# Final normalisation gathered behind the pair loop, score transposes behind the weighting, more value pairs split in an attention kernel

## What is computed

```python
H_l = H @ W_l
H_r = H @ W_r
S = H_l @ H_r.T                  # 4096 x 4096
beta = softmax(S, axis=-1)
B = beta @ H
O = B @ W_h @ W_g
x = layernorm(x + adj @ H + gamma * O)   # H is x
```

## Time and profile before

| | us |
|---|---|
| median of 3 executions | 1307.47 (1305.02 to 1307.64) |
| the profiled execution, its own time | 1307.26 |
| its span in the profile | 1305.4 |
| PE busy | 1259.0 (96%) |
| DVE busy | 958.2 (73%) |
| ACT busy | 800.9 (61%) |
| POOL busy | 233.7 (18%) |
| GpSimd remainders `ring_lo`, 64 | 155.4 |
| exponentials, 128 | 134.2 |
| rounded weights `p_hi` (L897), 64 | 67.9 |

### The profile page before, as it was taken

How to read it: one execution, slowest core, us unless ns; L and a number is a source line. 1 busy time by engine, 2 the same in 40 slices (tenths; PEclk the granted TensorE clock), 3 DMA queues, 4 the chain that set the end, 5 groups by cost and what they waited for, 6 DMA issues and landing times.

```text
span 1305.4 us, 17888 instructions
## 1 busy us (share of the span) xinstructions
PE 1259.0 (96%) x6139; PEld 829.7 (64%) x6139; DVE 958.2 (73%) x1265; ACT 800.9 (61%) x966; POOL 233.7 (18%) x136
## 2 busy tenths in 40 slices
PE   8999999989999899999999999999999999999987
PEld 3566666643332334788888888886677776767764
DVE  7987987720000556899999898978878888878885
ACT  1334555511110224788888777867978778788795
POOL 0100000000000000001010000012334333354355
PEclk9999999989999899999999999999999999999999
DMA  9877766589999699999999999960000000000000
GB/s 366 317 272 295 288 238 241 206 334 354 359 344 409 251 390 388 311 369 386 371 379 367 366 352 382 363 248 1 1 1 1 1 1 1 1 19 15 1 1 32
DMA packets 82816, 294.33 MB, mean 225 GB/s; under 512 B 9658, under 2 KB 11322, under 8 KB 82746
## 3 DMA queue, kind: packets, MB, share of 16 engines
q1 hardware_dynamic: 80496, 292.59, 59.7%
q10 hardware_dynamic: 2250, 0.82, 0.2%
HBM read 291.27 MB, written 2.10 MB: 225 GB/s over the span
## 4 chain that ended last, share of the span: by engine, by line
PE 85%; DVE 6%; DMA 4%; ACT 3%; issue 2%; DVEq 0%; SPq 0%; ACTq 0%
PE acc L1612 9%; PE acc L1607 9%; PE acc L1608 9%; PE acc L1694 8%; PE acc L1546 8%; DMA raw<-in_adj_s 4%; PE acc L1460 4%; PE acc L1452 3%; PE acc L1456 3%; PE acc L1453 3%; PE acc L1684 2%; PE acc L1688 2%; PE acc L1685 2%; PE rs L1469 2%; PE e L1649 2%; PE rs L1651 2%
## 5 line engine op out<-in xcount | busy, mean ns | idle before, releaser
L1161 DVE TENSOR_TENSOR t_lo<-raw,t_hi 128x1024 fp32r<-128x1024 f32 x256 | 303.2, 1230 | 21.6 <-ACT t_hi L847 18.2
L847 ACT ACTIVATE t_hi<-raw 128x1024 fp32r<-128x1024 f32 x256 | 261.5, 1054 | 38.0 <-PE acc L1612 36.9
L1607 PE MATMUL acc<-t_hi,st_hi 128*128 128x512 f32 x512 | 201.9, 394 | 0.6 <-ACT t_hi L847 0.6
L1608 PE MATMUL acc<-t_hi,st_lo 128*128 128x512 f32 x512 | 199.6, 390 | 0.0
L682 POOL TENSOR_TENSOR ring_lo<-ring,p_hi 128x1024 fp32r<-128x1024 f32 x64 | 155.4, 2429 | 231.3 <-ACT p_hi L897 231.2
L1612 PE MATMUL acc<-t_lo,st_hi 128*128 128x512 f32 x512 | 158.9, 392 | 1.4 <-DVE t_lo L1161 1.1
L1246 DVE TENSOR_TENSOR ring<-ring,e 128x1024 f32<-128x1024 f32 x128 | 153.9, 1210 | 0.1
L891 ACT ACTIVATE ring<-ring 128x1024 f32<-128x1024 f32 x128 | 134.2, 1054 | 23.1 <-DVE ring L1246 22.6
L637 POOL COPY xb<-x 128x512 f32<-128x512 f32 (+1 forms) x24 | 32.3, 1345 | 588.5 <-DVE xs L1079 214.8
L1694 PE MATMUL acc<-ring,x 128*128 128x512 f32 x256 | 120.4, 592 | 0.0
L1612 PEld LDWEIGHTS acc<-t_lo,st_hi 128*128 128x128 f32 x512 | 95.0, 188 | 24.6 <-DVE t_lo L1161 4.8
(11 more groups left out here) (228 smaller groups left out, 2181.2 us busy)
## 6 DMA issues: line engine op xcount, KB each, us to landing
raw<-in_adj_s SPq DMA_DIRECT2D x518, 512.0 KB, 5.6
kept_t<-in_adj_s SPq DMA_DIRECT2D x8, 512.0 KB, 7.2
x<-in_x SPq DMA_DIRECT2D x4, 512.0 KB, 9.2
kept_l<-in_adj_s SPq DMA_DIRECT2D x4, 512.0 KB, 7.3
kept_s<-in_adj_s SPq DMA_DIRECT2D x4, 512.0 KB, 6.5
kept_v<-in_adj_s SPq DMA_DIRECT2D x4, 512.0 KB, 6.6
kept_e<-in_adj_s SPq DMA_DIRECT2D x4, 512.0 KB, 8.5
kept_late<-in_adj_s SPq DMA_DIRECT2D x4, 512.0 KB, 11.1
```

The source lines that it names most:

```text
L847: nc.scalar.activation(t_hi[:, g % HL, :], raw[:, k, :], ACT.Copy).then_inc(hi_done, 1)
L1161: nc.vector.tensor_tensor(t_lo[:, k, :], raw[:, slot_no(s, c, g), :], t_hi[:, k, :].bitcast(F32), ALU.subtract).then_inc(lo_done, 1)
L1607: mm(a[:, :], block_of(st_h, b), hi[:, m], start=(g == 0 and j == 0), stop=False)
L1608: mm(a[:, :], block_of(st_l, b), hi[:, m], start=False, stop=False)
```

## The change

- **Which pairs are split.** In the first six query chunks 12 of 16 pairs (all k that are no multiple of 4), in the last two the same 8 as before: 88 in all, not 64. `p_hi` gets a third buffer (`NPH`).
- **Value remainders.** 12 instead of 8 values are split; ACT's `values_hi` run in ticks 11 to 22. The remainders are computed by POOL, nine ahead of its first `weights_lo`, three among the first of them. The remainders of odd k overwrite `x` in place, those of k = 2, 6, 10, 14 go over the first two chunks of `v`.
- **End of a query chunk.** PE does the weighting ahead of the transposes and of `peak_row`; DVE does `maximum` ahead of `diagonal`.
- **Last normalisation.** Nothing of it is left in the loop. After the loop's last tick blocks 0 to 27 are done together: six by ACT, 14 by DVE, eight by ACT behind its last copy `bt`; blocks 28 to 31 (the last chunk) by DVE and ACT, two each. The result is written over `xf`, in five transfers.

```diff
-SPLIT = tuple(range(1, KP, 2))
+SPLIT = tuple(k for k in range(KP) if k % 4)
+HALF = tuple(range(1, KP, 2))
+SPLIT_PAIRS = [n for n in range(NT) if n % KP in (SPLIT if n // KP < GQ - 2 else HALF)]
+NPH = 3
...
-        LN_PARTS = ((0, 16), (16, 24), (24, NB))
-        LN_SCALES = (NT - 34, NT - 4)
...
+        LN_PARTS = ((0, NB - CB), (NB - CB, NB))
+        ACT_FIRST, DVE_FIRST, ACT_SECOND = (0, 6), (6, 20), (20, NB - CB)
+        DVE_LAST, ACT_LAST = (NB - CB, NB - 2), (NB - 2, NB)
...
# GpSimd
+            def values_lo(j):
+                k = SPLIT[j]
+                pool.wait_ge(vh_done, j + 1)
+                if k % 2 == 0:
+                    pool.wait_ge(q_mm, 2)
+                nc.gpsimd.tensor_tensor(value_lo(k), x[:, 2 * k * D:2 * (k + 1) * D],
+                                        v_hi[:, j, :].bitcast(F32), ALU.subtract).then_inc(vl_done, 1)
...
+            for j in range(min(NSPLIT, 9)):
+                values_lo(j)
             for n in range(NT):
-                if n % KP in SPLIT:
+                if 9 <= n + 7 < NSPLIT:
+                    values_lo(n + 7)
+                if n in SPLIT_PAIRS:
                     weights_lo(n)
-                if n in POOL_LN:
-                    normalise_first(*POOL_LN[n])
...
# ScalarE
-                    if m > 1:
-                        act.wait_ge(pv_mm, split_pair(m - 2) + 1)
-                    nc.scalar.activation(p_hi[:, m % 2, :], slot(n), ACT.Copy).then_inc(ph_done, 1)
+                    if m >= NPH:
+                        act.wait_ge(pv_mm, SPLIT_PAIRS[m - NPH] + 1)
+                    nc.scalar.activation(p_hi[:, m % NPH, :], slot(n), ACT.Copy).then_inc(ph_done, 1)
...
-                if t in LN_SCALES:
-                    last_deviation(LN_SCALES.index(t))
...
             ticks(tick)
+            last_deviation(0)
+            last_norm(0, *ACT_FIRST)
             evacuate_weighted(GQ - 1)
-            last_deviation(2)
-            last_norm(*LN_LAST[1:])
+            last_norm(0, *ACT_SECOND)
+            last_deviation(1)
+            last_norm(1, *ACT_LAST)
...
# VectorE
-                if t % KP == 0 and 0 < t <= NT:
-                    diagonal(t // KP - 1)
                 if t < NT:
                     maximum(t)
+                if t % KP == 0 and 0 < t <= NT:
+                    diagonal(t // KP - 1)
...
-                if 12 <= t < 12 + NSPLIT:
-                    values_lo(t - 12)
...
             ticks(tick)
+            last_variance(0)
+            last_scales(0)
+            last_norm(*DVE_FIRST)
             finish_sums(GQ - 1)
...
# TensorE
+                if 0 <= t - LAG < NT:
+                    weighted(t - LAG)
                 if t % KP == 0 and 0 < t <= NT:
                     transpose_peak(t // KP - 1)
                 if t % KP == 1 and 1 < t <= NT + 1:
                     peak_row(t // KP - 1)
-                if 0 <= t - LAG < NT:
-                    weighted(t - LAG)
```

More of the change, by code:

```diff
@@ L227, in build @@
         ones_d = sb("ones_d", [P, 1])
+        with ExitStack() as last:
+            x_lo_v = sb("x_lo_v", [P, NB * D], F32R, last)
         x = sb("x", [P, NB * D])
@@ L232, in build @@
             kept_v = sb("kept_v", [P, 4, TW], F32, narrow)
+        with ExitStack() as last:
+            v_lo_more = sb("v_lo_more", [P, KP // 4, 2 * D], F32R, last)
         v = sb("v", [P, NB * D])
@@ L278, in build @@
             k_lo = sb("k_lo", [P, N - CW], F32R, att)
-            p_hi = sb("p_hi", [P, 2, PW], F32R, att)
+            p_hi = sb("p_hi", [P, NPH, PW], F32R, att)
             v_hi = sb("v_hi", [P, NSPLIT, 2 * D], F32R, att)
-            v_lo = sb("v_lo", [P, NSPLIT, 2 * D], F32R, att)
             peak = sb("peak", [P, PW], F32, att)
@@ L332, in build @@
          bt_done, out_mm, lrec_done, lg_done, o1_done, o2_done, sa_done, mva_done, fin_ve,
-         fin_std, fin_rc, fin_nmr, fin_x, fin_xa, fin_xp, l_mm) = (sem(n) for n in (
+         fin_std, fin_rc, fin_nmr, fin_x, fin_xa, l_mm) = (sem(n) for n in (
             "wt_mm wt_done wt_mean wt_scaled wt_centred qk_mm qk_done q_mm q_hi_done "
@@ L337, in build @@
             "bt_done out_mm lrec_done lg_done o1_done o2_done sa_done mva_done fin_ve "
-            "fin_std fin_rc fin_nmr fin_x fin_xa fin_xp l_mm").split())
+            "fin_std fin_rc fin_nmr fin_x fin_xa l_mm").split())
         def cols(t, c, width=CW):
@@ L605, in _ @@
             for a, b, by, count in RESULT:
-                sp.wait_ge({"fin_x": fin_x, "fin_xa": fin_xa, "fin_xp": fin_xp}[by], count)
-                sp.dma_start(out[:, a * D:b * D], v[:, a * D:b * D]).then_inc(out_done, 16)
+                sp.wait_ge({"fin_x": fin_x, "fin_xa": fin_xa}[by], count)
+                sp.dma_start(out[:, a * D:b * D], xf[:, a * D:b * D]).then_inc(out_done, 16)
             sp.wait_ge(out_done, 16 * len(RESULT))
@@ L681, in weights_lo @@
                 pool.wait_ge(ph_done, m + 1)
-                nc.gpsimd.tensor_tensor(ring_lo[:, n % RING, :], slot(n), p_hi[:, m % 2, :].bitcast(F32),
+                nc.gpsimd.tensor_tensor(ring_lo[:, n % RING, :], slot(n), p_hi[:, m % NPH, :].bitcast(F32),
                                         ALU.subtract).then_inc(pl_done, 1)
@@ L1302, in tick @@
                     subtract(t - SUB_AT)
+                if t < NT:
+                    maximum(t)
                 if t % KP == 0 and 0 < t <= NT:
                     diagonal(t // KP - 1)
-                if t < NT:
-                    maximum(t)
                 if t == 1:
@@ L1330, in _ @@
             finish_stats(GQ - 1)
-            last_variance(2)
-            last_scales(2)
-            last_norm(*LN_LAST[:2])
+            last_variance(1)
+            last_scales(1)
+            last_norm(*DVE_LAST)
         @block.tensor
@@ L1682, in weighted @@
                     for u in range(2):
-                        vh, ph = block_of(v_hi[:, j, :], u), p_hi[:, m % 2, u * CW:(u + 1) * CW]
+                        vh, ph = block_of(v_hi[:, j, :], u), p_hi[:, m % NPH, u * CW:(u + 1) * CW]
                         mm(o, vh, ph, start=(k == 0 and u == 0), stop=False)
-                        mm(o, block_of(v_lo[:, j, :], u), ph, start=False, stop=False)
+                        mm(o, block_of(value_lo(k), u), ph, start=False, stop=False)
                     pe.wait_ge(pl_done, m + 1)
```

41 lines of the change are left out of this document (11 added, 30 removed).

## The result

The changed kernel takes 1293.63 us (median of 4 runs, 1292.71 to 1294.79), the kernel before 1307.41 (1305.02 to 1307.64): a ratio of 0.990, 95% interval 0.989 to 0.992. The forecast was 1294.8. The profiled execution took 1292.71, with a span of 1290.8.

What follows compares the result with a forecast made beforehand. PE's own work was taken to bound the loop's middle; -8.4 + 0.5 - 3.6 - 1.5 + 0.8 - 0.5 = -12.7 us gave a median of 1294.8, with an eight-in-ten range of 1291.9 to 1301.5.

Steps and rivals of the forecast that it cites:

- Term 1: First six chunks: 24 more split pairs save 0.35 each on PE, -8.4 us, with +0.5 for lags.
- Term 4: Beginning of the weighting: extra roundings on ACT, partly offset by DVE losing value remainders, +0.8 us, bounds 0 and 2.7.
- Term 2: Ticks 94 and 124: square roots leave the loop, so PE's waits of 2.50 and 1.11 go, -3.6 us.
- Term 3: Start of the drain: earlier fold gains -1.5 us, with PE then waiting about 0.9 for POOL at pair 111.
- Term 5: The end: load and blocks fit into ACT's idle time before `bt`, and the last blocks take less, -0.5 us.
- ACT paces: First six chunks: ACT's steps don't overlap and set the pace, 4.8 us more, 1299.6; chance 0.17.
- POOL in DVE's way: Chunk's fold: POOL's remainders slow DVE's operation, up to 7.8 us more, 1302.6; chance 0.07.
- The beginning and the lags cost nothing: Beginning and lags free, fold's gain whole: 0.8, 0.5 and 0.9 more gained, 1292.6; chance of more gain 0.09.
- The pairs deliver nothing: PE waits for split pairs' rounding or remainder; only terms 2, 3 and 5 remain, 1301.9 to 1303; chance 0.06.
- Slower: Later `peak_row` delays subtractions, maxima and ACT; six chunks could lose 26 from the forecast, 1321; chance 0.04.

Runs made afterwards that it cites:

- old_order: Changed kernel with transposes and row ahead of the weighting, and the reduction ahead of the maximum, as before the change: 1301.62 us, ratio 0.994.
- norm_alone: Kernel before the change with only the final normalisation changed, moved behind the loop: 1301.62 us, ratio 0.995.
- loads_back: Changed kernel with a one-column square root put into ScalarE's queue at ticks 94 and 124, bringing the table loads back: 1300.70 us, ratio 0.994.
- values_early: Changed kernel with ScalarE's roundings of the values in ticks 7 to 18 instead of 11 to 22: 1293.14 us.
- two_buffers: Changed kernel with two buffers of rounded weights (NPH = 2) instead of three: 1308.81 us, ratio 1.001.
- all_chunks: Changed kernel with 12 of 16 pairs split in all eight chunks (8 more): 1297.35 us, ratio 0.992.
- old_pairs: Changed kernel with the old choice of pairs, 8 of 16 in every chunk, and 8 value pairs split by GpSimd: 1298.45 us, ratio 0.992.
- values_dve: Changed kernel with the value remainders computed by VectorE again, twelve in ticks 12 to 23: 1293.67 us.

## Why the prediction was right, point by point

**Term 1** was too large by its own number and right in place. Each pair is worth 0.35 on PE, and from the kernel before to the one after, folds came from 50.37 to 49.06 apart: 1.31 of 1.40, 0.45 lost in five chunks. The prediction had +0.5 for this lag. Taken away alone the 24 pairs bring 6.45, because the beginning's cost (term 4) belongs to them.

**The step behind it that failed** is "in a chunk without this the fold ends 3.2 after the scores": it took that number over from the kernel before. After the change it is 4.14, since ACT copies the last scores 0.74 after they end (1046.75 to 1047.49), with an exponential in front of them, and DVE takes the maximum 0.44 behind the copy, with a subtraction in front. The prediction worked out this very lag ("ACT falls 0.7 behind") and did not carry it to the fold. PE has three times 1.37 = 4.1 to do ahead of its transposes in the new order, so the late fold is just covered, with nothing to spare: the transposes begin 0.06 behind its end, as they do in old_order where they wait for it (1053.65 to 1053.70). In the old order PE has 2.7, and 4.15 - 2.74 = 1.41 is what each chunk loses in old_order. The forecast of 49.0 came out because the reorder, to which the prediction gave a gain only in the drain, paid for it: 7.9 in the loop. That part of the agreement is luck.

**The third buffer** was named as the condition (without it ACT would wait for a pair two or three back), with no price. It is 14.1 in the loop: more than the kernel gains.

**Term 2** (-3.6) holds. The two waits are gone in norm_alone (3.9 behind pair 25) and in the changed kernel, and come back as 2.41 and 0.99 in loads_back. What the prediction did not have is a cost behind such a wait, 1.6 once. The prediction's decision against a drain behind a table load holds too: an ACTIVATE starts 0.01 to 0.02 behind the end of each load shown above (1149.22 to 1149.24, 1276.85 to 1276.87). The page ScalarE: Activation LUTs of the Trainium skill, in "What ACT_TABLE_LOAD costs", has half of a switch's price as such a drain; these rows don't show it, and `bt` was not late. (With it the sum would have been 1.4 - 0.5 = 0.9 higher by the prediction's own figures, not 1.0.)

**Term 3** (-1.5) measured -1.35, by the steps that it named: fold 3.32 behind the last scores, forecast 3.21; wait for POOL at pair 111 0.90 from start to start, forecast 0.9; lost at the fold 0.29, forecast 0.1. From start to start 2.66 - 0.29 - 0.90 = 1.47, 0.12 more than the stretch gained; nearly all of that lies behind pair 111, where the way from the next pair to `bt` is 26.75 before and 26.85 after.

**Term 4** (+0.8) measured +0.67: pair 25's last scores matmul starts at 51.62 before and 51.94 after, 0.32 later where 0.35 earlier was counted (scores 26 start 0.32 later, forecast about 0.45). values_early shows that the late roundings on ACT are what costs it. POOL's value remainders took 0.73 to 0.81 each, not 0.6.

**Term 5** (-0.5) measured -0.53, with 0.58 to spare before `bt`, forecast 0.5. The 0.77 at the output transfers I had left at nothing. norm_alone has it too: from its last arithmetic to the end of the span are 2.35, as in the changed kernel, so it came with the smaller last pieces (128 KB twice, not 320 and 192). In two_buffers, with the same pieces, it was 2.97, so it is not there every time.

The sum of terms 1, 2 and 4 by measured parts is -8.4 + 0.45 - 3.6 + 0.67 = -10.9, against -11.08 in the trace. What the forecast lacks of the -14.6 in the span is the transfers and the 0.87 ahead of the attention part, which is chance: the code there is the same.

**The rivals.** *ACT paces*: fell. (Its price was also too high: by its own numbers four ticks are 3 x 3.12 + 2.06 = 11.4, not 11.5, which is 0.1 for each group, 2.6 in all and not 4.8.) Its waits for subtractions are 20.0 us in 36 places, longest 1.3, not more than the earlier trace rows:

```profile
ACT ring L897 <- DVE ring L1247: 20.0, 36, 1.3
```

*POOL in DVE's way*: fell in the loop, where every fold takes 0.69. It is real in the drain, where it costs nothing as long as DVE is early. POOL and DVE in the drain:

```profile
1263.68 2.40 POOL L686 TENSOR_TENSOR ring_lo<-ring,p_hi 128x1024 fp32r<-128x1024 f32 x1 [0.60 <-ACT p_hi L903]
```

```profile
1264.87 1.76 DVE L1263 TENSOR_TENSOR xf<-o_s,xf 128x512 f32<-128x512 f32 x1
```

The other additions into `xf` take 0.69. This one ends 0.55 behind that remainder, as the exclusion that the Trainium skill states (SBUF — State Buffer, "Who interferes with whom") would have it; in all_chunks the same shows at `nmr_a`. The other way round it is POOL that pays. Here the addition, of 0.69 from 1222.55, is the first to start, and the remainder takes 2.74, not 2.40:

```profile
1222.78 2.74 POOL L686 TENSOR_TENSOR ring_lo<-ring,p_hi 128x1024 fp32r<-128x1024 f32 x1 [4.77 <-ACT p_hi L903]
```

*The beginning and the lags cost nothing* gave 1292.6, within the scatter of the median, but its parts are refuted: beginning, lag and POOL's wait are all in the trace. *The pairs deliver nothing* fell with old_pairs. *Slower* fell: no wait for a maximum stands in the middle of the loop. The place where the kernel could have lost everything was the buffer, not `peak_row`.

## What to carry to other kernels

When work is made denser on the engine that bounds, the slack of every hand-over goes down with it: work out the new distance between producer and consumer at each of them instead of taking it over from the old trace, since an order and a buffer that are worth next to nothing at the old density (folds 50.37 apart in the kernel before, 50.31 with both in old_pairs) can be worth most or all of the gain at the new one. Parts of a change that are worth something only together should be taken away one at a time, as here order (8.6), buffer (14.1) and pairs (6.5), whose sum is far over the total. And in a part of the program where one engine's other work is absent, such as a drain, the balance of the loop does not hold: there the same pattern ran into POOL and ACT.

## What the hardware showed that I had not expected

A wait of PE of about 2 us sometimes costs more than its length: right behind it the granted clock of TensorE fell to half for some 3.4 us. In norm_alone, PE's timeline and the busy time by stretches (as above) show:

```profile
907.10 1.03 PE L1645 MATMUL e<-ident,folded_peak 128*128 128x128 f32 x4 [1.94 <-DVE folded_peak L1218]
...
908.35 0.63 PE L1638 MATMUL rs<-q_lo,k_hi 128*128 128x512 f32 x1
908.78 0.63 PE L1639 MATMUL rs<-q_hi,k_lo 128*128 128x512 f32 x1
```

```profile
904.00:908.00 4.00, 2.06 (x10) 1.50 (x10) 3.34 (x5) 2.41 (x4) 0.00 (x0) 0.90 0.00 0
908.00:912.00 4.00, 4.00 (x16) 3.14 (x16) 2.37 (x4) 1.27 (x2) 0.00 (x0) 0.67 0.01 2
912.00:916.00 4.00, 2.42 (x10) 1.44 (x9) 4.00 (x6) 3.45 (x5) 0.00 (x0) 1.00 0.00 0
```

Scores matmuls start 0.43 apart, elsewhere 0.23: the clock is at its lower level, 1.2 GHz, and not at 2.4. Six of them took 2.71 instead of 1.5, 1.2 lost. In loads_back it followed the wait of 2.41:

```profile
1154.58 0.63 PE L1649 MATMUL rs<-q_hi,k_hi 128*128 128x512 f32 x1
...
1155.86 2.78 PE L1694 MATMUL acc<-ring,x 128*128 128x512 f32 x4
```

Six scores matmuls took 2.20 instead of 1.47 and the unsplit weighting up to the next matmul 2.62 instead of 1.71: 1.64 lost. old_order has it behind a wait of 1.93 (granted clock 0.70 from 916 to 920, 0.87 from 920 to 924), and all_chunks at the end, where it fell within a wait of 2.25 and the `bt` sums behind took 1.86 instead of 1.05; the whole stretch from `bt` to the end of its span became 11.3 instead of 9.7. (At the very end the clock is low in every trace, but in the changed kernel only from 1284.87, behind these sums.) It is not there behind the waits of 2.50 and 2.49 of the kernel before, nor behind one of 1.94 there at 907.83, the same place and length as in norm_alone, nor behind one of 1.96 in values_dve. So it is no fixed price of a wait of this length, and why it falls in some executions and not in others stays open. By these traces, removing a wait of about 2 us can be worth up to 1.6 more than the row of that wait says.
